# A gated delta-rule layer with experts: grams of a chunk computed per head and spread by DMAs through HBM instead of by masks and selector matmuls

## What is computed

```python
q, k, v = silu(dwconv(x @ W_ + ...))          # three projections, causal convolution of 4 taps
a = sigmoid(x @ Wa + ba); beta = sigmoid(x @ Wb + bb)
def step(S, t):                               # S: per head 128 x 128, ks = k * SCALE
    y = einsum('bhvk,bhk->bhv', S, k_t)
    err = y - v_t
    S = a_t[..., None] * S - (b_t[..., None] * err)[..., None] * k_t[:, :, None, :]
    o = einsum('bhvk,bhk->bhv', S, q_t)
o = layernorm(o) * sigmoid(x @ Wg);  x = x + o @ Wo
x = x + mixture_of_8_experts_top2(layernorm(x)) + shared_expert
```

## Time and profile before

| | us |
|---|---|
| median of 3 runs | 3099.22 (3096.09 to 3100.3) |
| span of the profiled execution | 3102.6 |
| PE busy | 2732.2 (88%) |
| DVE busy | 2239.8 (72%) |
| ACT / POOL busy | 1610.3 / 1377.8 |

### The profile page before, as it was taken

The page is one execution under the profiler, slowest core; times in us unless marked ns, Lnnn a source line. Parts: engine busy times, 40 slices in busy tenths (PEclk is TensorE's granted clock), DMA queues, the critical chain, the costliest instruction groups (busy, mean ns, idle before and its releaser), DMA issues. The chain is left out here.

```text
span 3102.6 us, 48417 instructions
## 1 busy us (share of the span) xinstructions
PE 2732.2 (88%) x14144; PEld 1863.5 (60%) x14144; DVE 2239.8 (72%) x4680; ACT 1610.3 (52%) x3516; POOL 1377.8 (44%) x1760
## 2 busy tenths in 40 slices
PE   7999999768898888988889888898888888859999
PEld 3555555446666666666666666666666666635555
DVE  6777777677888878888788887888887888623332
ACT  6666666545555555555555555555555555412111
POOL 3666676734544445444454444544445444310000
PEclk9999999989999999999999999999999999979999
DMA  3655556533232232322323223232223222034120
GB/s 124 241 225 206 233 230 239 196 82 67 43 57 42 44 65 47 57 42 43 64 49 57 42 44 59 53 57 42 44 51 61 46 53 43 9 107 109 45 38 14
DMA packets 449883, 261.22 MB, mean 84 GB/s; under 512 B 402672, under 2 KB 414672, under 8 KB 447472
## 3 DMA queue, kind: packets, MB, share of 16 engines
q1 hardware_dynamic: 449664, 258.51, 31.5%
HBM read 153.42 MB, written 105.05 MB: 83 GB/s over the span
## 5 line engine op out<-in xcount | busy, mean ns | idle before, releaser
L265 DVE SCALAR_TENSOR_TENSOR A_acc<-A_psY,A_w,A_acc 128x410 f32<-128x410 f32 (+1 forms) x720 | 419.2, 637 | 151.6 <-ACT A_acc L334 151.6
L405 PE MATMUL A_psY<-A_xT,A_w 128*128 128x413 f32 (+1 forms) x960 | 347.2, 510 | 9.1 <-PE A_psAG L411 7.7
L1244 ACT ACTIVATE B_PQ<-B_psM 128x64 f32<-128x64 f32 (+2 forms) x480 | 125.2, 261 | 441.2 <-DVE B_NC L1137 440.9
L1137 DVE TENSOR_TENSOR B_NC<-B_NC,B_psM 128x256 f32<-128x256 f32 x480 | 200.8, 418 | 182.5 <-PE B_psM L1756 92.8
L192 POOL TENSOR_TENSOR A_outs<-A_outs,A_acc 128x410 f32<-128x410 f32 (+1 forms) x240 | 229.7, 987 | 216.1 <-ACT A_outs L342 216.1
L899 POOL TENSOR_TENSOR B_WT<-B_WT,B_G 128x128 f32<-128x128 f32 (+2 forms) x224 | 143.4, 640 | 371.2 <-ACT B_WT L1244 184.3
L1244 ACT ACTIVATE B_WL<-B_psT 64x128 f32<-64x128 f32 (+3 forms) x480 | 148.5, 309 | 265.6 <-PE B_psT L1723 265.4
L405 PEld LDWEIGHTS A_psY<-A_xT,A_w 128*128 128x128 f32 x960 | 180.2, 189 | 165.5 <-issue 164.2
L1140 DVE TENSOR_REDUCE B_W<-B_NC 128x64 f32<-128x320 f32 x512 | 248.7, 486 | 17.6
L334 ACT ACTIVATE A_acc<-A_psY,A_w 128x410 f32<-128x410 f32 (+1 forms) x240 | 166.1, 692 | 162.9 <-PE A_psY L405 161.2
L879 POOL TENSOR_TENSOR B_PQ<-B_PQ,B_G 128x256 f32<-128x256 f32 x128 | 89.4, 699 | 345.5 <-DVE B_WT L1105 345.5
(11 more groups left out here) (207 smaller groups left out, 6588.4 us busy)
## 6 DMA issues: line engine op xcount, KB each, us to landing
B_KQ<-scr SPq DMA_DIRECT2D x96, 512.0 KB, 6.6
scr<-A_outs SPq DMA_DIRECT2D x48, 615.0 KB, 3.5
scr<-A_outag SPq DMA_DIRECT2D x32, 615.0 KB, 5.2
scr<-A_outs SPq DMA_DIRECT2D x48, 409.0 KB, 2.5
A_xc<-nbeta SPq DMA_DIRECT2D x16, 1024.0 KB, 5.9
B_A<-scr SPq DMA_DIRECT2D x32, 512.0 KB, 4.6
B_C<-scr SPq DMA_DIRECT2D x32, 512.0 KB, 6.3
B_G<-scr SPq DMA_DIRECT2D x32, 512.0 KB, 4.6
```

The lines of the kernel that those rows point to most:

```text
L265: nc.vector.scalar_tensor_tensor(a, y, w[:, s, col:col + 1], a, ALU.mult, ALU.add)\
L405: last = nc.tensor.matmul(psY[p][:, y0:y0 + HALO + t1 - t0], wp[:, p, kt, :], xT[:, kt, t0:t1 + HALO], start=kt == 0, stop=kt == KT - 1)
L1137: tt(eq[:, :, :, 1:5], eq[:, :, :, 1:5], left.unsqueeze(2).to_broadcast([128, H, R, R]), ALU.mult)\
L1244: copy = lambda out, in_: nc.scalar.activation(out, in_, ACT.Copy)
```

## The change

All masks, selectors, sorted copies and the decay transposes go. For each chunk PE now computes 16 plain grams, one per head (64 keys by 64 tokens of KB and Q, interleaved: 128 columns), in four jobs (`gram` 0 to 3, at leaves 0 to 2 of the chunk before). ACT copies them to GR and SP stores GR to the HBM tensor gram_d. Then SP issues, per chunk, 41 DMAs from HBM to HBM that cut pieces out of gram_d: `place_keys` 12 (one element of 4 B per packet, 128 elements each), `place_blocks` 8 + 8 + 2 + 1 (runs of 32, 64, 128 and 256 B; 64, 64, 256 and 512 rows), `place_rows` 10 (4 B, 256 elements each). The block images lie zeroed in HBM beforehand, so their off-diagonal stays zero. They are loaded to BD and OWN (`load_blocks`), and the rows by loads that repeat one row in all 128 partitions (`load_keys` 6 KB a partition, `load_rows` 10 KB). The decays of the state go to HBM as 2048 single elements (`store_decays`) and come back as a broadcast of 8 KB a partition (`load_decays`). `place_keys`, `place_blocks` and `place_rows` wait for gram_d to have landed, `load_keys` for all 31 DMAs of keys and blocks.

```diff
 def short_jobs(g, j):
-        2: [("own", 1, 1)],
+        2: [("gram", 2)] if g + 1 < NCH else [],
         3: [("ktok", 0)],
-        8: ([("own", 0, 0)] if not last else []),
-        10: [("gram", 5)],
-        14: ([("wo", 1)] if wo else []),
+        13: [("wo", 1)] if wo else [],
 def leaf_jobs(g, j):
-        -1: [("gram", 2), ("gram", 3)],
-        0: ([("qk", 0, 0), ("qk", 0, 1)] if out else []),
-        1: [("own", 1, 0)],
-        2: [("gram", 1)],
-        3: ([("qk", 1, 0), ("qk", 1, 1), ("qk", 2, 0), ("qk", 2, 1)] if out else []),
-        4: [("kk", 1, 0), ("kk", 1, 1), ("gram", 4)],
+        0: ([("gram", 0)] if not last else []),
+        1: ([("gram", 1)] if not last else []),
+        2: ([("gram", 3)] if not last else []),
+        4: [("ktok", 1)],
...
-        9: [("decay", 1)],
...
-        13: [("decay", 2), ("decay", 3)],
@@ sync
+            def store_grams(c):
+                wait(sp, grc, c, 4)
+                if c:
+                    wait(sp, ost, c, 0)
+                sp.dma_start(gram_d.rearrange("(n p) c -> p n c", p=128), GR[:]).then_inc(grs.sem, 16)
...
+                for half in range(2):
+                    for k, (s, t) in enumerate(KEY_PAIRS):
+                        sp.dma_start(at(key_d, (half * NKEY + k) * HJ2, (J // 2, H), (1, J // 2)),
+                                     at(gram_d, (half * C // 2 + s) * row + half * C + 2 * t + at_p(c), (head, H), (R * (row + 2), J // 2)),
+                                     allow_slow_non_contiguous=True).then_inc(bst.sem, 16)
...
+            def load_keys(c):
+                wait(sp, bst, c + 1, 0)
+                wait(sp, ncs, 2 * c, 0)
+                sp.dma_start(LK[:].rearrange("p l k x -> p (l k x)"), key_d.rearrange("l k h j -> (l k h j)").partition_broadcast(128))\
+                  .then_inc(kld.sem, 16)
...
             for g in range(NCH):
+                load_blocks(g, 1)
+                store_decays(g)
+                if more:
                     wait(sp, awm, g - 1, 6)
                     wait(sp, nl, 2 * g - 1, 3)
-                    load("A", n, at)
+                    load("A", (g + 1) % 2, (g + 1) * C)
                 if g:
                     wait(sp, og, g - 2, 4)
                     load("G", 0, (g - 1) * C)
-                if g + 1 < NCH:
+                if more:
+                    store_grams(g + 1)
+                if g + 2 < NCH:
+                    wait(sp, ktok, g, 2)
+                    for what in ("K", "KB", "Q"):
+                        load(what, g % 2, (g + 2) * C)
+                load_rows(g)
+                if more:
+                    wait(sp, grs, g + 2, 0)
+                    place_keys(g + 1)
+                    place_blocks(g + 1)
+                    place_rows(g + 1)
                     wait(sp, nc0, 2 * g + 1, 5)
-                    load("C0", n, at)
+                    load("C0", 0, (g + 1) * C)
+                    load_keys(g + 1)
+                load_decays(g)
+                if more:
+                    load_blocks(g + 1, 0)
@@ vector: row_pairs
-                wait(dve, nlc, i, 2)
-                ps = take_two_banks(dve, g if h else g - 1, "kk", h)
+                wait(dve, kld, g, 1)
+                wait(dve, ncs, i - 1, 0)
@@ vector: chunk
-                    elif j == 2:
-                        mask_own(g, 1, 0)
-                        mask_own(g, 1, 1)
...
                     elif j == 12:
+                        decay_state(g, 0)
@@ scalar: pairs_copy
-                ps = take_two_banks(act, g if h else g - 1, "kk", h)
+                wait(act, kld, g, 1)
```

More of the change, by code:

```diff
@@ L489, in pair_number, with gram_place @@
     return j // 2
[L492 to L502, removed]
+def gram_place(j, i):
+    p, n, _ = merge_of(j)
+    m = j // (2 << p)
+    if p == 1:
+        return (m, 6 + m)[m // 2]
+    if p == 2:
+        return 8 * m + 2 + i
+    return 4 + i
 def recurrence(nc, ident, scr, nbeta_d, wo_d, lng_d, lnb_d, att_d):
@@ L521, in recurrence @@
         center = sb("center", [128, 128])
-        causal = sb("causal", [128, 3, 128])
-        source = sb("source", [128, 2 * R])
+        dram = lambda name, shape: nc.dram_tensor(name, shape, FP32).ap()
+        gram_d, decay_d = dram("gram", (H * C, COLS)), dram("decay", (H, D))
+        block_d, own_d = dram("block", (sum(SETS), TILE)), dram("own", (J // 2, 64, 128))
+        key_d, out_d = dram("key", (2, NKEY, H, J // 2)), dram("rows", (2, NOUT, H, J))
         KQ = sb("KQ", [128, 2, 3, H, C])
@@ L663, in take_bank @@
             return ring[b]
-        def two_banks(*job):
-            b, _ = place[(*job, 0)]
-            return banks[:, b:b + 2]
-        def take_two_banks(eng, *job):
-            for leaf in range(2):
-                b, k = place[(*job, leaf)]
-                eng.wait_ge(full[b], k)
-            return two_banks(*job)
         FQ = SQ[:].rearrange("p h c -> p (h c)")
@@ L721, in _ @@
             for what in ("A", "K", "KB", "Q"):
                 load(what, 0, 0)
-            load("C0", 0, 0)
+            wait(sp, zeros, 0, NZERO)
+            zero = WX[:].rearrange("p k x -> p (k x)")
+            part = sum(SETS) * TILE // 256
+            for k in range(2):
+                sp.dma_start(at(block_d, k * part, (2 * part, 128), (1, part)), zero[:, 0:part]).then_inc(cl.sem, 16)
+            sp.dma_start(at(own_d, 0, (512, 128), (1, 512)), zero[:, 0:512]).then_inc(cl.sem, 16)
@@ L724, in _ @@
+            load("C0", 0, 0)
+            store_grams(0)
+            wait(sp, grs, 1, 0)
+            place_keys(0)
+            place_blocks(0)
+            place_rows(0)
+            load_keys(0)
+            load_blocks(0, 0)
+            for what in ("K", "KB", "Q"):
+                load(what, 1, C)
             sp.dma_start(wo[:], wo_d).then_inc(wol.sem, 16)
@@ new lines, in shared_job @@
+                elif kind == "gram":
+                    loaded(pe, "K", g + 1)
+                    loaded(pe, "KB", g + 1)
+                    loaded(pe, "Q", g + 1)
+                    kq = KQ[:, (g + 1) % 2]
+                    for m in range(2):
+                        for l in range(2):
+                            h = 4 * n + 2 * m + l
+                            last = mm(ps[64 * l:64 * (l + 1), COLS * m:COLS * (m + 1)], kq[:, 0, h, :],
+                                      kq[:, 1:3, h, :].rearrange("p x t -> p t x"), start=True, stop=True)
```

460 lines of the change are left out of this document (153 added, 307 removed).

## The result

The changed kernel takes 4441.55 us (median of 4 runs, 4411.69 to 4462.16), the kernel before on the same chip 3097.65. The ratio is 1.432, 95% interval 1.426 to 1.438: 43% slower. The direction of the forecast holds; the time lies 1020 us above the forecast 3421 and above the range, which ended at 4000.

The account below looks back on a forecast made before the run. The leaf chain through DVE, PE and ACT bounded the kernel; SP's chain to LK would lengthen it. Period 32 + 42.9 = 74.9 us: 3102.6 + 308 + 20 - 6, less 3.4, gives 3421 us; range 3290 to 4000.

Parts of the forecast that it names:

- S: Time from G's issue through SP's DMAs until LK has landed for row_pairs(nxt): 32 us.
- b': Rest of the changed loop, from row_pairs(nxt) to the next G: 42.9 us, bounds 41 to 44.
- a: In the kernel before, the distance from G's issue to row_pairs(nxt), leaves 6 to 11: 21.5 us.
- Steps 3 and 4: SP issues 31 DMAs of keys and blocks, then 10 of rows and C0; 0.38 us an issue, done by 24.
- Steps 3 to 5: Small DMAs, C0 and load_keys drain in SP's queue at 30 ns per 4 B packet; LK issued at 24.5, landed at 32.
- my signs: Profile after: SP waiting long ahead of LK for landed DMAs would show the packet price wrong; closer issues, step 3's issue price.
- small packets bound the chain: Rival: neighbouring 4 B writes drain slowly, 40 to 88 ns a packet, S 36 to 54.5, total 3550 to 4120 us; chance 0.28.
- The consumers: At leaf 11, DVE's row_pairs(nxt) waits for LK, and ACT's pairs_copy(nxt) stands ahead of the copy WL that PE needs.
- The 3 us gained a chunk: DVE loses 8 mask products a chunk, 5.5 us; about half counted as gain in an otherwise unchanged schedule.
- The start: Before the first leaf: grams, copy, store, 41 issues and keys landed at 656 make the start some 20 us later.
- The 6 us that I had credited at the end: Last chunk prepares nothing and gains 3 us; the selector matmuls behind it give another 3.

Follow-up runs that it names:

- e1: Kernel before, with 41 small HBM-to-HBM DMAs added on SyncE behind each chunk's C0 load, into a tensor nobody reads: 3123.67 us, ratio 1.009.
- e9: Changed kernel with LK loaded from scratch (other values), and C0, LK and decays issued ahead of the 41 small DMAs: 3630.11 us, 1.172.
- e3: Changed kernel with the 10 DMAs of place_rows replaced by one of the same bytes in contiguous runs (other values in LQ): 3797.48 us, 1.224.
- e2: Changed kernel with the 10 place_rows DMAs moving the same bytes in contiguous 64 B runs (other values in LQ): 3990.63 us, 1.287.
- e5: Changed kernel with place_rows writing each 4 B element to 256 B of its own (other values in LQ): as fast as with 64 B runs.
- e12: Changed kernel, SyncE reordered (keys and LK early, K/KB/Q and rows late), row and key elements reordered, decays stored in 64 B runs: 3336.67 us, 1.077.
- e16: e12 with four PSUM ring banks and one extra 128x512 matmul on PE at the end of each leaf: 3346.00 us, 1.079.
- e14: Changed kernel with four PSUM ring banks and the y terms' first operand from the freed bank (other values): 4371.74 us.
- e18: e12 with four PSUM ring banks and first operands of y terms and row-pair products from PSUM (other values): 3316.93 us, 1.070.
- e17: e12 with four PSUM ring banks and one extra 128x256 matmul on PE at the end of each leaf: 3352.60 us, 1.082.

## Why the prediction was wrong in size

In a chunk the forecast 74.9 us became 106.8: 27.4 of the 31.9 us are S, 4.4 are b'. In S, LK was issued at 39.1 us on average (forecast 24.5) and landed 20.4 us later (forecast 7.5). Step by step, by the terms of the prediction:

- **The mechanism was right.** `row_pairs(nxt)` waits for LK at leaf 11, LK stands behind G in SP's program, and S takes the place of a. e1 (3124 us with such transfers, nobody waiting) shows that the loss is in the waiting. But it isn't in this one wait: without the wait for the keys and with LK ahead of the small DMAs e9 is still 17% slower, since A waits in its place.
- **Steps 3 and 4, the issue price: failed in size.** I took 0.38 us from issues of DMAs between SBUF and HBM. The new ones take 0.60 us each (rows: 520/608/632 ns min/median/max), and the 41 need 26.8 us from 1563.70 to 1590.5 where I had 15.6: 11.2 us a chunk. e3 confirms the price, 5.9 us for nine. The Trainium skill's sentence that initiating a DMA is usually small beside the DMA itself (page "DMA: Bandwidth & Descriptors", section "Issuing engines are not separate DMA queues"), which the prediction weighed, is true of one of them here (0.61 us of 12.2) and misleads for 41 in one queue.
- **Steps 3 to 5, the drain: failed.** I priced a 4 B packet at 30 ns in its DMA engine and put the landing of LK at 7.5 us behind its issue. LK lands after 20.4 us at the median, 22 in the chunk shown. The 7.5 us are near what LK takes where the rows are written in runs or far apart (7.6 in e2, 7.7 in e5); the drain adds 13.8 us a chunk to S by e2. A record says 9 ns, but the packets of the rows lie 84 ns apart in each engine, and the loads behind them are slow too. Of my signs, SP waiting long ahead of LK was to show a wrong packet price; it issued LK at once, and the landing took the time. The rival "small packets bound the chain" named the cause, many 4 B writes in the same few hundred bytes, at 0.28; e5, which moves them apart, shows it. The rival's upper price of 88 ns a packet was near the 84. But it kept the issue price of 0.38 us, so its upper end (54.5 us for S) was still below the 59.4 measured, and the range below the time.
- **The consumers: one missed.** ACT waits for C0 at leaf 10, 1187.5 us in all, behind the same DMAs. It ends before LK does, so it cost nothing more here; but any cure must move both.
- **The 3 us gained a chunk, and b' = 42.9: wrong in sign.** I credited DVE's removed masks. Outside leaf 11 the leaves are 4.3 us longer. What the runs show of it: the granted clock of PE falls from 0.99 to 0.68, in part in the stall itself (0.50), but also without it (0.79 in e12), since the removed work had also kept PE busy (e16 makes leaves on the chain 0.3 to 0.7 us shorter); and products that read PSUM now read SBUF, where they hold up POOL and are held up by it (e14, e18: 0.5 to 0.9 us in leaf 4). Cured one at a time, neither moved the total by more than 0.6%; other leaves or waits grew by as much. How the 4.3 us divide between them and the order of work stays open.
- **The start.** 20 us forecast, 43.7 measured: the first leaf's product begins at 686.28 for 642.56 before, by the same two terms: the 41 issues take 26.4 us from 636.18, and LK, issued at 662.60, is there at 680.10, where I had 656.

The terms add up: 31 x (106.8 - 64.95) = 1297, and 43.7 at the start, 1341 of the 1345.3 us between the two spans. The 6 us that I had credited at the end are not among them.

How far a cure goes is shown by e12: with SP's order turned round and single elements kept apart, 1105 of the 1344 us are gone. None of the versions beats the kernel before; the best with the full computation is 7.6% slower. The best that could be hoped for by the table is the 65 us of the other leaves and a leaf 11 of 4.3, an estimate of 69 us a chunk, still above 64.95.

## What to carry to other kernels

Where a dependency is moved to HBM and back, count the DMAs, not the bytes: each costs its issue in the one ordered queue, and loads behind it that have nothing to do with it wait too. Single elements written side by side are the dearest form: store whole runs, or order the elements so that neighbours aren't written in a row, and put what is urgent ahead. A short record of each packet doesn't say that they are cheap: look at how far apart they come and at what stands behind them. Before crediting the removal of work beside the chain, ask whether it kept a clock up or an operand out of SBUF.

## What the runs showed of the hardware

- A DMA of 256 elements of 4 B, HBM to HBM, landed after 12.2 us when the elements went side by side (10 such DMAs in a row), 6.7 with the same elements in another order, 2.3 when each went to 256 B of its own, and 1.9 as runs of 64 B.
- While such writes drain, each 4 B packet is recorded with 9 ns, but the packets lie 84 ns apart in an engine, and the following load is recorded as slow (256 B packets of 60 ns on average for 18; 58 GB/s at a share of 0.87 for 12 us, then 386 GB/s).
- The issue of such a DMA of 256 elements took SyncE 520/608/632 ns (min/median/max), for 325 ns of a store from SBUF.
- PE's granted clock over the steady part was 0.79 with PE 76% busy (e12), 0.86 with 83% (e17), 0.95 with 85% (e16) and 0.99 with 88% (before), a mixture of stretches at 1.2 and at 2.4 GHz.
- A POOL product took 1.53 us beside a DVE product with two SBUF operands and 0.68 beside one with a PSUM operand.
- With four banks instead of five in the PSUM ring the changed kernel was 56 us faster (LK landed 0.8 us sooner after its issue); why was not tried.
